# Graph attention on one core: value projections spread over the opening, and a new order of work where the opening hands over to the main loop

## The reference, cut to what matters

```python
h = relu(layernorm(x))                        # x: 4096 x 512
q, k, v = h @ Wq.T + bq, h @ Wk.T + bk, h @ Wv.T + bv
z = (q @ k.T) / sqrt(512) * adj               # adj: 4096 x 4096, zeros and ones
z = where(z == 0, -10000, z)
out = x + relu(softmax(z, axis=1) @ v)        # 4096 x 512
```

## Time and profile before

| | |
|---|---|
| median of three runs | 1510.57 us |
| the profiled execution, its own time | 1511.22 us |
| its span | 1509.4 us |
| TensorE matmul, busy | 1481.5 us (98%) |
| TensorE weight load, busy | 943.5 us (63%) |
| VectorE, busy | 1273.4 us (84%) |
| ScalarE, busy | 879.8 us (58%) |
| chain that ended last | PE 92%, DVE 3%, issue 2%, DMA 1%, ACT 1% |
| moved by DMA | 304.92 MB, mean 202 GB/s |

### The profile page before, as it was taken

How to read it: one execution, slowest core, us unless ns; L and a number is a source line. 1 busy time by engine, 2 the same in 40 slices (tenths; PEclk the granted TensorE clock), 3 DMA queues, 4 the chain that set the end, 5 groups by cost and what they waited for, 6 DMA issues and landing times.

```text
span 1509.4 us, 24873 instructions
## 1 busy us (share of the span) xinstructions
PE 1481.5 (98%) x9550; PEld 943.5 (63%) x9550; DVE 1273.4 (84%) x1570; ACT 879.8 (58%) x1402; POOL 1.7 (0%) x11
## 2 busy tenths in 40 slices
PE   8899999889999999999999999999999999999998
PEld 4456665556666666666666666666666666666544
DVE  5978886888897889888988898889978897988875
ACT  2566665665566556565656555655665566555542
POOL 0000000000000000000000000000000000000000
PEclk9999999999999999999999999999999999999999
DMA  5255544475554656556656665566556655664252
GB/s 202 99 207 204 181 155 164 167 283 210 217 216 182 249 213 226 210 222 227 219 201 237 237 226 196 211 237 238 209 210 221 229 210 209 215 220 185 86 168 84
DMA packets 75526, 304.92 MB, mean 202 GB/s; under 512 B 8464, under 2 KB 8464, under 8 KB 73616
## 3 DMA queue, kind: packets, MB, share of 16 engines
q1 hardware_dynamic: 75408, 303.33, 54.8%
HBM read 264.51 MB, written 38.80 MB: 201 GB/s over the span
## 4 chain that ended last, share of the span: by engine, by line
PE 92%; DVE 3%; issue 2%; DMA 1%; ACT 1%; SPq 0%; POOLq 0%; DVEq 0%; POOL 0%; ACTq 0%
PE o L559 44%; PE za L503 22%; PE zd L503 11%; PE zb L503 5%; PE o L490 4%; PE o L476 4%; PE o L458 1%; DVE stats L954 0%; DMA o_rows<-in_x 0%; DMA g_buf<-g_dram 0%; DMA g_dram<-spare 0%; PE za L587 0%; ACT g_buf L724 0%; DVE h_buf L1003 0%; DVE half_min L990 0%
## 5 line engine op out<-in xcount | busy, mean ns | idle before, releaser
L559 PE MATMUL o<-v_buf,p_buf 128*128 128x512 f16 x3072 | 736.5, 380 | 3.3 <-issue 3.3
L559 PEld LDWEIGHTS o<-v_buf,p_buf 128*128 128x128 f16 x3072 | 300.9, 98 | 273.0 <-issue 5.2
L503 PE MATMUL za<-h_buf,g_buf 128*128 128x256 f16 x2976 | 407.6, 273 | 7.5 <-DVE g_buf L1029 3.4
L503 PEld LDWEIGHTS za<-h_buf,g_buf 128*128 128x128 f16 x2976 | 290.4, 98 | 145.7 <-DVE g_buf L1029 5.1
L503 PE MATMUL zd<-h_buf,g_buf 128*128 128x256 f16 x1488 | 203.6, 273 | 0.0
L1093 DVE TENSOR_TENSOR slots<-um_tmp,dm_tmp 128x512 f32<-128x512 f32 x128 | 88.4, 691 | 111.7 <-ACT dm_tmp L774 111.6
L1140 DVE TENSOR_TENSOR p_buf<-slots,p_buf 128x1024 f16<-128x1024 f32 x128 | 156.1, 1220 | 21.7 <-PE o L559 20.1
L786 ACT ACTIVATE slots<-slots,log_p 128x1024 f32<-128x1024 f32 x128 | 145.9, 1140 | 37.3 <-DVE slots L1133 37.3
L781 ACT ACTIVATE slots<-za,c_all,kappa 128x256 f32<-128x256 f32 x128 | 72.4, 565 | 145.5 <-PE za L503 144.7
L503 PEld LDWEIGHTS zd<-h_buf,g_buf 128*128 128x128 f16 x1488 | 146.0, 98 | 17.2
L1105 DVE SCALAR_TENSOR_TENSOR slots<-slots 128x1024 f32<-128x1024 f32 x128 | 156.0, 1219 | 0.2
(11 more groups left out here) (151 smaller groups left out, 1107.4 us busy)
## 6 DMA issues: line engine op xcount, KB each, us to landing
g_buf<-g_dram SPq DMA_DIRECT2D x112, 896.0 KB, 5.4
v_buf<-v_dram SPq DMA_DIRECT2D x128, 512.0 KB, 3.4
adj_own<-in_adj SPq DMA_DIRECT2D x91, 512.0 KB, 6.2
spare<-in_adj SPq DMA_DIRECT2D x37, 512.0 KB, 6.3
g_dram<-g_buf SPq DMA_DIRECT2D x12, 896.0 KB, 4.7
v_dram<-v_buf SPq DMA_DIRECT2D x16, 512.0 KB, 5.2
spare<-in_x SPq DMA_DIRECT2D x15, 512.0 KB, 8.8
h_buf<-h_dram SPq DMA_DIRECT2D x7, 1024.0 KB, 8.8
```

The source lines that it names most:

```text
L503: mm = pe.matmul(bank[:, 0:QH], g_of(i)[:, a, op, j, :], right[b][j], start=(fresh and j == 0 and m == 0), stop=(j == 1 and m == 2), skip_ ...
L559: mm = pe.matmul(o_bank[t][:, :], a[:, kt, span], v_buf[:, n % V_BUFS, kt, b, :], start=(j == 0 and kt == 0 and m == 0), stop=(j == PAIRS ...
```

## The change

- A table `V_PARTS` says in which parts a value is projected: parts 11, 15, 19, 23, 27, 29, 35 and 37 have none, and the last projection is in part 39. `v_tile(k)` is the tile of part k, or -1. In a part without a projection `transpose_h` stands in its place, between pieces 0 and 1 of the pair begun.
- Halves of quads 4 to 7 are kept in other buffers: quad 7 in `o_rows`, block 1's h and its sums change places, the stage for the sums of block 1 is `p_buf`. `high_h` waits for the value projection of the tile whose place it takes.
- Block 1's h is read back in part 25 instead of 28, `combine_t(1)` runs in parts 28 to 31 (was 32 to 35), `high_t(1)` in 30 to 33 (was 36 and 37), `low_t(1)` in 31 to 34 (was 37 and 38).
- ScalarE runs a [128, 1] exponential in part 36. `square_root` comes behind `normalise` and `copy_g` in its part.
- The seventh product of a pair has its own semaphore, `zc_ready`.
- SyncE's order follows the parts: a value store comes one part behind its second tile, `store_g` in parts with i = 1, and `load_g(16)` at part 40, behind `store_v(15)`. It waits only for the stores of its own places.
- Behind the opening the order on all engines is new. `turn_min` comes before piece 3 of pair 17, `widen_min` before piece 1 of pair 18, and piece 0 of pair 19 before piece 3 of pair 18. VectorE has `columns_min` ahead of `add_c11(17)` and `negate(16)`. ScalarE does `copy_floor` ahead of `copy_u2(18)`, `exp(0)` ahead of `copy_u4(18)`, and `exp(1)`, `high_p(1)` only in step 0.

```diff
+PARTS = QUAD * (QUADS + 2) + 1
+NO_V = (11, 15, 19, 23, 27, 29, 35, 37)
+V_PARTS = [k for k in range(PARTS) if k not in NO_V][:TILES]
...
-            for g in range(QUADS + 2):
-                if 1 <= g < QUADS:
+            for k in range(PARTS + 1):
+                g, i = k // QUAD, k % QUAD
+                if i == 0 and 1 <= g < QUADS:
                     store_h(g)
...
+                if k - 1 in V_PARTS and v_tile(k - 1) % 2 == 1:
+                    store_v(v_tile(k - 1) // 2)
+                if i == 1 and 2 <= g < QUADS + 2:
                     store_g(2 * (g - 2))
                     store_g(2 * (g - 2) + 1)
-                if g == QUADS - 1:
+                if k == 25:
                     load_h(1)
...
+                if opening_pair(k - 2) >= 0 and opening_pair(k - 2) + 2 < PAIRS:
+                    load_adj(opening_pair(k - 2) + 2)
+                if k == PARTS - 1:
+                    load_g(PAIRS)
-            for u in range(G_OPEN):
-                sp.wait_ge(g_stored[u], 16 * PAIRS // G_OPEN)
-            load_g(PAIRS)
+            sp.wait_ge(g_stored[G_OPEN - 1], 16 * PAIRS // G_OPEN)
             load_g(PAIRS + 1)
...
@@ tensor, opening
-                if g < QUADS:
-                    project_v(k)
+                if v_tile(k) >= 0:
+                    project_v(v_tile(k))
+                elif g + 1 < QUADS:
+                    transpose_h(k + QUAD)
                 if begun >= 0:
                     scores(begun, 1)
                 if ended >= 0:
                     scores(ended, 3)
-                if g + 1 < QUADS:
+                if v_tile(k) >= 0 and g + 1 < QUADS:
                     transpose_h(k + QUAD)
...
@@ tensor, handover
-            for i in (PAIRS, PAIRS + 1):
-                for piece in range(4):
-                    scores(i, piece)
+            for piece in range(4):
+                scores(PAIRS, piece)
+            for piece in range(3):
+                scores(PAIRS + 1, piece)
             turn_min(0, o_bank[2])
+            scores(PAIRS + 1, 3)
             scores(PAIRS + 2, 0)
+            widen_min(0, o_bank[3])
             scores(PAIRS + 2, 1)
-            widen_min(0, o_bank[3])
             scores(PAIRS + 2, 2)
+            scores(PAIRS + 3, 0)
             scores(PAIRS + 2, 3)
...
@@ scalar
+                if 30 <= k < 34:
+                    high_t(1, k - 30)
+                if k == 36:
+                    act.wait_ge(ones_ready, 2)
+                    nc.scalar.activation(exp_first[:, :], log_p[:, :], ACT.Exp)
...
+            copy_m1(PAIRS + 2)
+            copy_m2(PAIRS + 2)
+            copy_floor(0, o_bank[3])
+            copy_u2(PAIRS + 2)
+            copy_m7(PAIRS + 2)
+            exp(0)
+            copy_u4(PAIRS + 2)
+            copy_d(PAIRS + 2)
+            high_p(0)
...
@@ vector, handover
             add_c11(PAIRS)
+            halve_min(0)
             add_c2(PAIRS)
-            halve_min(0)
             weigh(PAIRS)
+            columns_min(0, o_bank[2])
             add_c11(PAIRS + 1)
             negate(PAIRS)
-            see_min(PAIRS)
             add_c2(PAIRS + 1)
-            columns_min(0, o_bank[2])
             weigh(PAIRS + 1)
+            lower(0)
             add_c11(PAIRS + 2)
             negate(PAIRS + 1)
-            lower(0)
+            see_min(PAIRS + 1)
             add_c2(PAIRS + 2)
+            low_p(0)
             lower(1)
```

More of the change, by code:

```diff
@@ L297, in opening_pair, with v_tile @@
             return pair if i % 2 == 1 and 0 <= pair < PAIRS else -1
-        PARTS = QUAD * (QUADS + 2) + 1
+        def v_tile(k):
+            return V_PARTS.index(k) if k in V_PARTS else -1
         block = ctx.enter_context(nc.Block())
@@ L545, in scores @@
                     pe.wait_ge(u4_copied, i + 1)
-                    product(i, a, S4, of_h(s, 1, 1), False).then_inc(za_ready, 1)
+                    product(i, a, S4, of_h(s, 1, 1), False).then_inc(zc_ready, 1)
             def weigh_v(n, t):
@@ L656, in _ @@
                 more = n + LEAD < STEPS
-                if more:
+                if more and n > 0:
                     scores(n + LEAD, 0)
@@ L850, in _ @@
                     high_m(3)
-                if g < QUADS:
-                    high_v(k)
+                if v_tile(k) >= 0:
+                    high_v(v_tile(k))
                 if begun >= 0:
@@ L875, in _ @@
                     copy_g(g - 1, i)
-            for n in range(-3, STEPS):
+                if i == 2 and g + 2 < QUADS:
+                    square_root(g + 2)
+            for i in (PAIRS, PAIRS + 1):
+                copy_m1(i)
+                copy_m2(i)
+                copy_u2(i)
+                copy_m7(i)
+                copy_u4(i)
+                copy_d(i)
+                copy_c12(i)
+            copy_m1(PAIRS + 2)
[7 more added lines that the diff above has]
+            high_p(0)
+            for n in range(STEPS):
                 s, j = n // PAIRS, n % PAIRS
-                first = j == PAIRS - 2 and 0 < s + 1 < BLOCKS
+                first = j == PAIRS - 2 and s + 1 < BLOCKS
                 more = n + LEAD < STEPS
-                soon = 2 <= n + 2 < STEPS
-                if PAIRS <= n + LEAD - 1 < STEPS:
+                soon = n + 2 < STEPS
+                if n + LEAD - 1 < STEPS:
                     copy_c12(n + LEAD - 1)
@@ L888, in _ @@
                     copy_m2(n + LEAD)
-                if soon and not first:
+                if n == 0:
+                    exp(1)
+                elif soon and not first:
                     exp(n + 2)
@@ L895, in _ @@
                     copy_floor(s + 1, a_bank[0])
-                if n == -1:
-                    copy_floor(0, o_bank[3])
-                if soon and not first:
+                if n == 0:
+                    high_p(1)
+                elif soon and not first:
                     high_p(n + 2)
-                if s >= 0 and s + 2 < BLOCKS:
+                if s + 2 < BLOCKS:
                     if j == 9:
@@ L910, in _ @@
                     copy_d(n + LEAD)
-                if n == -1:
-                    exp(0)
-                    high_p(0)
-                    exp(1)
-                    high_p(1)
-                if first:
+                if first or n == 0:
                     exp(n + 2)
                     high_p(n + 2)
-                if j == PAIRS - 1 and s >= 0:
+                if j == PAIRS - 1:
                     copy_o(s, 0)
@@ L1266, in _ @@
                     low_m(3)
-                if g < QUADS:
-                    low_v(k)
+                if v_tile(k) >= 0:
+                    low_v(v_tile(k))
                 if i == 2 and 1 <= g <= QUADS:
```

89 lines of the change are left out of this document (44 added, 45 removed).

## The result

The changed kernel takes 1515.75 us, the median of six runs (1514.52 to 1518.71). The kernel before, six runs beside it, takes 1510.65 us (1509.15 to 1512.25). The ratio is 1.0036, with a 95% interval of 1.0026 to 1.0046: **5.1 us slower**. The profiled execution took 1514.74 us, with a span of 1513.0, 3.6 us above that of before.

What follows compares the result with a forecast made beforehand. TensorE, never idle from 400 to 1480 us, bounds the kernel; the change is decided before 340 us. +4.5 +1.9 +0.9 -0.8 -2.9 = +3.6 on 1511.22 gives 1514.8, less 0.65 for the median: 1514.2; range 1506.0 to 1518.5.

Steps and rivals of the forecast that it cites:

- Spreading, up to A: Opening to the last key projection's end (A): stalls +7.3 us, projections -7.8, old waits -2.4; A at 283.4.
- Rival (c): Parts without value projection: VectorE isn't late, the 7.3 us of stalls shrink to 3, total 1510; chance 0.15.
- Pair 14: Ahead of pair 14 TensorE stalls 2.7 us instead of 3.40, then 0.7 and 0.5 for the next two pieces.
- The key load: Pair 16's load queues behind the last value store: TensorE waits 4.6 us instead of 1.0, +4.5 us.
- Rival (a): At pair 16 the key load isn't late, so TensorE goes through: 1506.9 us; chance 0.25.
- The clock behind the key load's wait, and the handover: Low clock behind pair 16's wait, +1.9 us; pair 16's first product to the first sums, -0.8 us.
- The clock behind pair 14's wait: Behind pair 14's 2.7 us wait, low clock costs nothing or 1.9 us with equal weight: +0.9 us.
- The clock before the first sums: The wait ahead of the first sums falls to 2.3 us, with no drop of the clock: -2.9 us.
- Rival (b): The clock falls before the first sums too, or behind pair 14 in full: +2.9 us, 1517; chance 0.22.
- The early table: In the handover, the table load moves into part 36 behind high_g, taking 1.28 us off the chain.
- Rival (d): At exp(0) the table is loaded again: +1.3 us, inside the main range; no chance given.
- The rest: Block 1's earlier sums, the fourth product's semaphore, the square root's place and sooner h loads: 0 us each.

Runs made afterwards that it cites:

- key_load_early: The changed kernel with load_g(16) issued two parts sooner, ahead of the last value store: 1510.91 us.
- after: The changed kernel itself, as profiled, against the kernel before: 1515.75 us, ratio 1.0036.
- same_again: The changed kernel run once more without an edit: 1515.99 us.
- all_three: The changed kernel with key projections and ScalarE's work moved earlier in parts without value projection, load_g(16) two parts sooner, g's halves first in part 36: 1508.58 us.
- no_spread_filled: The changed kernel with all value projections in parts 0 to 31, load_g(16) sooner, g's halves first in part 36, pair 19's piece 1 before the sums: 1504.61 us.
- old_handover: The changed kernel with the earlier kernel's order behind the opening on all three engines, early exponential kept: 1514.97 us.
- spread_less_table_late: As no_spread_filled, but parts 11, 27, 29, 32, 35 have no value projection, and part 36 no early exponential: 1503.82 us.

## Why the prediction was right, and which term was wrong

The direction, the mechanism and the largest term held. 5.1 us were measured, 3.6 forecast, inside the range (1514.2 forecast, 1515.75 measured). That the sum came so near is in part luck: a saving of 2.9 us at the first sums came to 1.2 in the second profile, a cost of 0.9 at pair 14 didn't come in either, and these errors point opposite ways. Step by step, the profile's times less the 1.46 us by which part 11 began later:

- **Spreading, up to A.** Predicted 283.4; the last key projection ends at 282.60 + 2.59 = 285.19, less 1.46 = 283.7. The prediction counted a hole from the time at which TensorE could have gone on. Counted so, part 19 has the predicted 1.6: piece 1 starts 163.93 - 160.58 = 3.35 us after the first product, where 1.31 + 0.44 = 1.75 is work. The idle times of the rows, 1.03 and 0.20, come to less, since a matmul's modelled end lies 0.16 behind the time at which the next could start (a product lasts 0.82 and takes 0.66). The holes are 0.6 in part 11, three of 1.6, 0.6, 0.9 and 1.1: 8.0 us against 7.3. Parts 29 and 35, at 0.7 each, were the ones taken too small; the two waits of the earlier trace rows that went were worth 2.7 in this count and not 2.4. Rival (c) is refuted: VectorE caught up nothing. Its `add_c11` starts 2.22 us after part 19's first product (160.58), and started 2.23 after it in before (162.07 and 164.30 in the earlier trace rows):

```profile
162.80 0.42 DVE L1126 TENSOR_TENSOR slots<-mm_tmp 128x256 f32<-128x256 f32 x1
```

- **Pair 14.** 2.7 us predicted, 2.61 measured; then 0.7 and 0.5 predicted, 0.53 and 0.23 measured.
- **The key load.** Issued at A + 21.5 (21.4 predicted), 5.79 us to the landing with 0.06 to the matmul (6.1 predicted), wait 4.02 (4.6 predicted). Pair 16 at 311.08, 310.9 predicted. key_load_early shows the cause: the wait and its low clock are gone and 5.1 us come back. The rule of the Trainium skill that the prediction named ("Perfetto Trace Analysis", "Per-instruction lifecycle"; a DMA instruction's semaphore wait is held in the sequencer of the issuing engine) holds in the trace: the load goes out 0.44 us behind the store in after, and 9 us ahead of it where it is written ahead. Rival (a) is refuted for this kernel; what it describes is what key_load_early measures, at 1510.91 us instead of 1506.9. The 4.0 us between them are, in its profile, 1.2 of a later part 11, 0.5 of a later pair 16, 0.6 of the handover, and 1.5 of the clock, which fell behind the wait before the sums; the rest is the distance of its median from its profile.
- **The clock behind the key load's wait, and the handover.** +1.9 and -0.8 predicted, +1.1 together. From pair 16 to the first sums after takes 21.25 us and same_again 22.25, before 20.87: +0.4 and +1.4. The low stretch lasted two windows in one and over three in the other. Where no such wait is ahead (key_load_early, all_three) the handover takes 20.68, so the new order with the early table is worth 0.2 us and not 0.8, and 0.7 at best. What I missed is a wait of 0.65 us for `copy_m1` in pair 17 where pair 16 comes without a pause. Where there is a pause at full clock (no_spread_filled) it takes 20.20.
- **The clock behind pair 14's wait.** +0.9, half of 1.9, predicted. Nothing in after, same_again, key_load_early and old_handover; it came with the same 2.61 us in the three kernels that kept this wait and had the key projections moved.
- **The clock before the first sums: the term that failed.** "This is nearer to 1.6 than to 3.3, so I take no drop of the clock: -2.9." The wait was 2.05 us (2.3 predicted), and in the profiled execution the clock held; that execution is among the fastest of the six. But it fell behind the very same wait in the second profile of the same kernel and in five of five edited kernels that kept it: six of seven. From the first sums to the end of the span before takes 1182.1 us, after 1179.2, and the six others 1180.7 to 1180.9. So the term is -2.9 where the clock holds and -1.2 to -1.4 where it falls, since the low stretch is shorter than that of before, and what was forecast for the median was the rare case. Rival (b), which said this for 1517, is half of the truth: the clock falls before the sums, but costs 1.5 to 1.7 us and not 2.9, and at pair 14 it didn't fall.
- **The early table.** Rival (d) is refuted: after has no table load at `exp(0)`. But it saved at most 0.2 us that the new order hadn't. The prediction set the 2.66 us of the Trainium skill ("ScalarE: Activation LUTs", "What ACT_TABLE_LOAD costs") beside the row's 1.28; where the load is put back the row has 1.28 again with the exponential 0.01 behind it, and the measurement decides.
- **The rest** was 0 as predicted, so far as TensorE's waits show.

The sum for the second profile, whose start lies 0.2 us behind that of before: +0.20 at part 11, +4.46 at pair 16, +1.38 to the sums, -1.24 behind them: +4.8, which is its span's difference. This is close to the median's 5.1. For after's own profile: +1.46, +4.66, +0.38, -2.90 = +3.6. Whether the start is later on average is open: among the thirteen profiles of changed kernels it lies between 98.93 and 100.59 us, and there is one of before.

## What to carry to other kernels

Walk each queue in the order written, with the time at which each entry's condition is met: a load that feeds the critical engine goes ahead of any store that waits for the last result. Moving work of one engine from a full stretch into a gap leaves holes behind wherever that work had covered the lateness of another engine; here eight small ones cost as much as the long ones that they replaced. Before an operation is counted as saved, look at how long the next engine on the path had to spare: here 0.48 us of 1.28. Compare holes by starts, since idle times between modelled ends come out short. A wait on TensorE has two prices, its length and the clock behind it. So filling a 2 us wait with work that is due soon anyway can return more than the wait.

## What the runs showed of the hardware that was not expected

**Whether the clock falls is not settled by the length of a wait near 2 us.** From part 11 to 345 us, the granted clock in the windows behind each wait:

| wait of TensorE, us | granted clock near 0.50 behind it |
|---|---|
| up to 1.8 | in no profile |
| 2.02 and 2.12 (pair 16's load) | not behind 2.02, but behind 2.12 |
| 2.05 (first sums) | in 6 profiles of 7 |
| 2.33 and 2.61 (pair 14) | not behind 2.33; in 3 of 7 behind 2.61 |
| 2.70 (first sums, old order) | yes |
| 3.3 to 4.2 | in all 7 |

Where TensorE waited 2 us or more ahead of pair 14 or pair 16, its last wait had ended 6 us or more before. Ahead of the first sums it is otherwise: the 2.05 us followed another wait, of 0.54 to 0.55 us, with a single product of 0.83 us between the two. Two profiles of the same program with the same waits went either way there (1.00 in after, 0.50 in same_again), so the waits alone don't decide, and these runs don't tell what does.

**A table load does not wait for the data of its activation.** It began at 318.02 in spread_less_table_late, right behind the copy ahead of it, while the subtraction that its activation needs ran from 317.92 to 319.1. So it can be hidden, all but 0.2 us of it here, in a wait for data without an early activation that brings it in.
